# A fused vision tower on one core: whole-tile DMAs for the token tiles, and a reordered tail of gates

## The chip, the cores and the metric

One Trainium2 chip, one of its cores. The time is device microseconds of one execution of the whole kernel; lower is better. Times of several executions are given as a median.

## The reference

The input holds coefficients C of shape (8, 256, 64, 2). Three stages follow one another, all in float32:

```python
h = _L0_tok_ref(x, log_dt, log_w_real, w_imag, 512)          # (8, 256, 512): 2*Re(Cm . exp(K)), a state-space kernel
h = h + _L0_attn_ref(_layernorm(h), w_q, w_k, w_v, w_o)      # 16 query heads, 4 key/value heads of 128, rope, causal
h = h + _L0_ffn_ref(_layernorm(h), select_weight, ...)       # per token one of 8 experts
```

The last stage, for every token and each of 8 experts, divides the squared products with `select_weight` by the squared length of the token minus `select_mean_diff`, passes the score through a sigmoid (the gate), takes the expert with the largest gate, and gives `(1 - gate) * x + gate * (bias + degen @ (upd @ (x - debias)))`.

## The kernel before

There are NB = 8 sequences ("batches") of S = 256 tokens with D = 512 channels. Tokens lie on partitions: a batch has TT = 2 token tiles of 128 tokens x 512 channels, and `x[:, t, b, :]` in on-chip memory is tile t of batch b. **The token order is not the plain one.** Partitions 0 to 63 of tile t hold tokens t*64 to t*64+63, partitions 64 to 127 hold tokens 128 + t*64 and on: `half_rows(hh)` names the partitions of a half and `tokens_of(hh, t)` its tokens. A half is contiguous in `out[b]`; a whole tile is two such runs, 64 tokens apart. In DRAM scratch, `x_dram`, a token's 8 batches stand side by side, so a row of 2 KB (512 float32) is the contiguous piece there.

**Mixing stage (to about 98 us).** Sixteen steps q make the state-space outputs: GpSimd and VectorE build factors, TensorE multiplies, ScalarE evacuates to one of two staging buffers `st[s]` (`evacuate`), and the sync engine writes them to `x_dram` (`store_mixed`, two transfers, line 463). `evacuate` waits until the store of the same buffer two steps earlier has landed (`xd_out[s]`). After the eighth step tile 0 of batch 0 is loaded back (`load_tokens`, line 467), and after each of the next seven steps tile 0 of one more batch; tile 1 of all eight batches follows once the sixteenth store has landed. `load_tokens(t, b, done)` issues two DMAs, one for each half. VectorE waits for `x_early`, `x_first`, `x_second`, `x_third` and `x_rest` before it takes the layer-norm statistics of the tiles they cover; `x_rest` covers batches 3 to 7, both tiles (`dve.wait_ge(x_rest, ...)` ahead of `norm_stats(tokens(3), 3)`, whose instruction is line 1202). Between the tile-1 loads of batches 2 and 3 stand two loads of the output weights (`load_raw(KC)`, `load_raw(KC + 1)`).

**Attention.** For each of 4 groups of heads, 8 batches: projections, rope, scores, softmax, values, output product, each float32 product made of three products of rounded parts (lines 1547 to 1549). Each engine has its own hand-written order of work, with semaphores between them.

**Gates and results.** In the last group's steps the gates of the earlier batches are made two steps behind, and `finish(bb)` (line 1391, VectorE) adds the last term to the two tiles of a result and raises `out_ready`. Results are stored by the sync engine, `store_tile` and `store_half` (line 387), two DMAs of 128 KB a tile, in one fixed order: first all loads of saved values (`load_vs`), then batches 0 to 5, tile by tile, then tiles of batch 7 and of batch 6, of which the sync engine stores the lower halves and ScalarE's queue the upper ones.

**Tail (from about 765 us).** The seventh and eighth batches' (bb = 6, 7) gates are made together in `late_both`, with 4 tiles' worth of columns. VectorE's order was: statistics and normalising of batch 7 tile by tile (`last_stats`, `last_apply`, the latter line 1513), with `finish(4)` for tile 0 between; `gate_choice(5)`; then, once TensorE has the products (`f_ready`), `read_gates` (three instructions, lines 1316 to 1319), `gate_scores` (lines 1339 to 1347), `finish(4)` for tile 1 while ScalarE makes the exponentials (line 931), and `gate_values` and `gate_choice` (lines 1360 to 1377). TensorE then transposes the choices and makes four update products (line 1683), and VectorE ends with two additions for batch 7 (line 1532) and six `finish` instructions. GpSimd makes the reciprocal roots of batch 7's two tiles (lines 739, 741) and then adds batch 5's scaled tiles (`add_scaled`, line 730). At the end the sync engine waits until every store has landed.

Of the kernel before, what the change touches and what calls it, by code (L numbers as in the profile page):

```python
# [25 lines left out]
P = 128  # L26
# [122 lines left out]
def tower(nc, mix_c, mix_s, log_dt, log_wr, w_im, w_qkv, w_o, w_gate, w_gmul, w_upd, centers, slopes, consts, out):  # L149
# [3 lines left out]
    with top:  # L153
# [223 lines left out]
        def half_rows(hh):  # L377

            return slice(hh * NS, (hh + 1) * NS)

        def tokens_of(hh, t):

            first = hh * P + t * NS
            return slice(first, first + NS)

        def store_half(engine, bb, t, hh):
            engine.dma_start(out[bb, tokens_of(hh, t), :], x[half_rows(hh), t, bb, :]).then_inc(stored, 16)

# [36 lines left out]
        def _(sp):  # L425
# [37 lines left out]
                    sp.dma_start(rows[q, hh], st[s][:, hh, :, :]).then_inc(xd_out[s], 16)  # L463

            def load_tokens(t, b, done):
                for hh in range(2):
                    sp.dma_start(x[half_rows(hh), t, b, :], x_dram[tokens_of(hh, t), b, :]).then_inc(done, 16)

            with sp.Fori(0, NQ // 4) as it:
                for s in range(2):  # L470
# [67 lines left out]
            load_vs(3, 1, 3)  # L538
            load_ffn()
            load_vs(3, 3, NB)  # L540
            def store_tile(bb, t, counted, halves=range(2)):
                sp.wait_ge(out_ready, counted)
                for hh in halves:
                    store_half(sp, bb, t, hh)

            with sp.Fori(0, NB - 2) as bb:
                for t in range(TT):
                    store_tile(bb, t, bb * 2 + (t + 1))
            for k, bb in enumerate((NB - 1, NB - 2)):
                for t in range(TT):  # L550
                    store_tile(bb, t, 2 * (NB - 2 + k) + t + 1, (0,))
            sp.wait_ge(stored, 16 * 2 * NB * TT)


        @block.gpsimd
        def _(pool):
# [171 lines left out]
            def add_scaled(bb, t):  # L728
                pool.wait_ge(xn_scaled, bb * 2 + (t + 1))
                nc.gpsimd.tensor_tensor(x[:, t, bb, :], x[:, t, bb, :], norm_set(NB + bb)["xn"][:, t, :],  # L730
                                        ALU.add).then_inc(xn_added, 1)

            normalise_probs(NG * NB - 1)
            norm(2 * NB - 2)
            for t in range(TT):
                mem = norm_set(2 * NB - 1)
                rstd = mem["rstd"][:, t:t + 1]
                pool.wait_ge(tile_var, t + 1)
                nc.gpsimd.tensor_tensor(rstd, mem["mv"][:, t, 1:2], cst[:, C_EPS:C_EPS + 1], ALU.add).then_inc(tile_eps, 1)
                pool.wait_ge(tile_eps, t + 1)  # L740
                nc.gpsimd.tensor_tensor(rstd, rstd, cst[:, C_POW:C_POW + 1], ALU.pow).then_inc(tile_rstd, 1)
            for t in range(TT):
                add_scaled(NB - 3, t)
            pool.wait_ge(x7_added, 2)
            for t in range(TT):
                add_scaled(NB - 2, t)
# [3 lines left out]
        def _(act):  # L750
# [253 lines left out]
            round_probs(last)  # L1004
            round_attn(last, 0)

            def scale_normed(bb):
                mem = norm_set(NB + bb)
                act.wait_ge(gate, bb * GATE + GATE_KEEP)
                for t in range(TT):  # L1010
                    nc.scalar.activation(mem["xn"][:, t, :], mem["xn"][:, t, :], ACT.Copy,
                                         scale=mem["one_minus"][:, t:t + 1]).then_inc(xn_scaled, 1)

            gate_exp(NB - 3)
            xt2(NB - 2)
            scale_normed(NB - 3)
            act.wait_ge(f_ready, NB - 1)
            for t in range(TT):
                act.wait_ge(xt_ready, 2 * (2 * NB - 1) + t + 1)
# [15 lines left out]
        def _(dve):  # L1035
# [226 lines left out]
                return v.tensor_tensor(columns_of_pair(xt_l, q, t), pair_of(bank), columns_of_pair(xt_h, q, t).bitcast(F32),  # L1262
                                       ALU.subtract)

            dve.wait_ge(x_early, 32)
            norm_stat(tokens(0), 0)
            wait_apart(dve, ln_st, 1, 4)
            v.bn_aggr(norm_set(0)["mv"][:, 0, :], stats[:, 0, :]).then_inc(early_var, 1)
# [2 lines left out]
            for q in range(2):  # L1271
                dve.wait_ge(early_hi, q + 1)
                half_rest(q, 0, 5 + q).then_inc(early_lo, 1)
            dve.wait_ge(x_first, 32)
            norm_stat(tokens(0), 1)
            wait_apart(dve, ln_st, 2, 4)
            v.bn_aggr(norm_set(0)["mv"][:, 1, :], stats[:, 1, :]).then_inc(ln_var, 1)
# [2 lines left out]
            for q in range(2):  # L1280
                dve.wait_ge(xt_hi, q + 1)
                half_rest(q, 1, (7, 3)[q]).then_inc(xt_lo, 1)
            dve.wait_ge(x_second, 64)
            norm_stats(tokens(1), 1)
            norm_apply(tokens(1), 1)
            def kq_rest(s, j):
# [2 lines left out]
                v.tensor_tensor(flat(kl), part(kq), flat(kh).bitcast(F32), ALU.subtract).then_inc(kq_lo, 1)  # L1289

            rope(0, 0)
            dve.wait_ge(x_third, 64)
            norm_stats(tokens(2), 2)
            rope(0, 1)
            rope_add(0, 0)
# [26 lines left out]
            def gate_link(bb, n):  # L1322

                def then(ins):
                    n[0] += 1
                    ins.then_inc(gate, 1)
                    dve.wait_ge(gate, bb * GATE + n[0])
                return then

            def bc(t, tiles):  # L1330
                return t.unsqueeze(2).to_broadcast([P, tiles, NE])
# [18 lines left out]
            def gates(bb, mem=None, tiles=TT):  # L1350
                gate_values(bb, mem, tiles)
                gate_choice(bb, mem, tiles)

            def gate_values(bb, mem=None, tiles=TT):

# [10 lines left out]
            def gate_choice(bb, mem=None, tiles=TT):  # L1366

                mem, n = mem or norm_set(NB + bb), [GATE_KEEP]
                then = gate_link(bb, n)
                z, rank, mm, best, first = mem["z"], mem["rank"], mem["mm"], mem["best"], mem["first"]  # L1370
                then(v.tensor_tensor(rank, z, bc(best, tiles), ALU.is_equal))
                then(v.tensor_tensor(rank, rank, cst[:, C_RANK:C_RANK + NE].unsqueeze(1).to_broadcast([P, tiles, NE]),
                                     ALU.mult))
                then(v.tensor_reduce(first, rank, AX.X, ALU.max))
                onehot = mm[:, :, 64:72]
                then(v.tensor_tensor(onehot, rank, bc(first, tiles), ALU.is_equal))
                v.tensor_tensor(mm[:, :, 0:64].rearrange("p t (n h) -> p t n h", n=NE),
                                mem["gm"].rearrange("p t (n h) -> p t n h", n=NE),
                                onehot.unsqueeze(3).to_broadcast([P, tiles, NE, HE]), ALU.mult).then_inc(m_ready, 1)
                assert n[0] == GATE, n  # L1380
# [93 lines left out]
            rope_add(1, 1)  # L1474
            probs_rest(0)
            rope(1, 2)
            dve.wait_ge(x_rest, 16 * 4 * 5)
            norm_stats(tokens(3), 3)
            rope_add(1, 2)
            norm_apply(tokens(3), 3)  # L1480
# [40 lines left out]
            finish(NB - 4, (2, 3), (0,))  # L1521
            last_apply(1)
            gate_choice(NB - 3)
            dve.wait_ge(f_ready, NB)
            read_gates(late_both, quad[:, 0:2, :].rearrange("p b (t c) -> p (b t) c", t=TT), 2 * TT)
            dve.wait_ge(f_read, NB - 1)
            gate_scores(NB - 2, late_both, 2 * TT)
            finish(NB - 4, (2, 3), (1,))
            gates(NB - 2, late_both, 2 * TT)
            mem = norm_set(2 * NB - 1)  # L1530
            for t in range(TT):
                v.scalar_tensor_tensor(x[:, t, NB - 1, :], mem["xn"][:, t, :], mem["one_minus"][:, t:t + 1],
# [412 lines left out]
```

## Time and profile before

| | us |
|---|---|
| median of 3 runs | 802.74 (802.38 to 805.21) |
| profiled execution, its own time | 801.88 |
| its span, first to last instruction | 800.0 |
| TensorE busy | 736.1 (92% of the span) |
| VectorE busy | 575.0 (72%) |
| ScalarE busy | 444.9 (56%) |
| GpSimd busy | 434.4 (54%) |
| mean granted TensorE clock | 0.994 of full speed |

The profiled execution is one run; what lies outside its span is 1.9 us. Times inside it are counted from the span's start. "SPq" and "ACTq" are the queues on which the sync engine and ScalarE issue DMAs; a transfer's issue there is short, and its data lands later. In the views of DMA, q1 is the sync engine's queue and q10 ScalarE's, and the share is that of the time of the core's 16 DMA engines.

### The profile page before, as it was taken

The page shows a single profiled execution, that of the slowest core. Times are in us where ns is not written, and L with a number is a line of the kernel's source. Part 1 is how long each engine was busy: PE and PEld are TensorE (multiplying, and loading weights), DVE is VectorE, ACT ScalarE, POOL GpSimd, SP SyncE. Part 2 cuts the span into 40 slices and gives each one's busy share as a digit, 9 for nine tenths or more (in the row PEclk, how much of TensorE's full clock was granted, in tenths as well). Part 3 has the DMA queues.
Part 4 walks back from the last instruction along what each step waited for, and adds up shares of the span by engine and source line. Part 5 has one row for each costly group of instructions (what it writes and reads, how often), then busy time and mean ns, then how long its engine had stood idle before and what let it go on. Part 6 is the DMA issues. An engine that isn't in the chain of part 4 may idle for free.

```text
span 800.0 us, 19498 instructions
## 1 busy us (share of the span) xinstructions
PE 736.1 (92%) x6902; PEld 671.3 (84%) x6902; DVE 575.0 (72%) x1604; ACT 444.9 (56%) x1236; POOL 434.4 (54%) x649
## 2 busy tenths in 40 slices
PE   0277788999999999999999999999999999999996
PEld 0166768999999999999989999999999998989883
DVE  7999877887765666766674565665666678888886
ACT  6735435665555667555674555555575655465431
POOL 1488866644444747544474564444384745665632
PEclk9999999999999999999999999999999999999999
DMA  9023741100010203000011020000020000000403
GB/s 217 6 56 79 178 138 34 54 8 2 7 47 8 67 8 99 7 7 7 7 29 39 1 93 8 7 7 1 8 68 7 29 8 8 7 7 13 100 1 105
DMA packets 38127, 31.59 MB, mean 39 GB/s; under 512 B 23790, under 2 KB 29294, under 8 KB 38070
## 3 DMA queue, kind: packets, MB, share of 16 engines
q1 hardware_dynamic: 37606, 30.25, 14.3%
q8 instruction: 35, 0.57, 0.3%
q10 hardware_dynamic: 464, 0.59, 0.3%
q14 instruction: 22, 0.18, 0.1%
HBM read 20.34 MB, written 10.49 MB: 39 GB/s over the span
## 4 chain that ended last, share of the span: by engine, by line
PE 81%; DVE 7%; POOL 4%; ACT 3%; issue 2%; DMA 1%; DVEq 0%; SPq 0%; ACTq 0%; POOLq 0%
PE bank_quad L1548 17%; PE bank_quad L1547 16%; PE bank_quad L1549 16%; PE bank_pair L1547 4%; PE bank_pair L1548 4%; PE bank_pair L1549 4%; PE bank_quad L1559 2%; PE bank_pair L1736 2%; PE bank_pair L1746 2%; PE bank_quad L1665 2%; PE bank L1746 2%; PE bank L1750 2%; PE bank L1547 2%; PE bank L1548 2%; PE bank L1549 1%
## 5 line engine op out<-in xcount | busy, mean ns | idle before, releaser
L1547 PE MATMUL bank_quad<-xt_hi,w_hi 128*128 128x256 f32 (+1 forms) x568 | 159.5, 281 | 0.0
L1548 PE MATMUL bank_quad<-xt_hi,w_lo 128*128 128x256 f32 (+1 forms) x568 | 158.9, 280 | 0.0
L1549 PE MATMUL bank_quad<-xt_lo,w_hi 128*128 128x256 f32 (+1 forms) x568 | 158.6, 279 | 0.0
L652 POOL TENSOR_TENSOR swap<-swap,cst 128x512 f32<-128x512 f32 (+1 forms) x96 | 105.5, 1110 | 38.4 <-ACT swap L885 38.3
L942 ACT ACTIVATE sm<-sm,mx 128x128 f32<-128x128 f32 (+1 forms) x256 | 113.6, 445 | 20.1 <-DVE mx L1406 20.1
L1249 DVE TENSOR_TENSOR kq<-kq,swap 128x512 f32<-128x512 f32 (+1 forms) x96 | 89.9, 957 | 25.9 <-POOL swap L652 24.8
L1547 PEld LDWEIGHTS bank_quad<-xt_hi,w_hi 128*128 128x128 f32 x568 | 106.8, 188 | 0.0
L1548 PEld LDWEIGHTS bank_quad<-xt_hi,w_lo 128*128 128x128 f32 x568 | 106.7, 188 | 0.0
L1549 PEld LDWEIGHTS bank_quad<-xt_lo,w_hi 128*128 128x128 f32 x568 | 106.3, 187 | 0.0
L692 POOL TENSOR_SCALAR sm<-sm,rinv 128x128 f32<-128x128 f32 (+1 forms) x256 | 103.9, 418 | 0.1
L954 ACT ACTIVATE ot_hi<-bank_quad 128x512 fp32r<-128x512 f32 x64 | 37.8, 597 | 118.4 <-PE bank_quad L1549 118.4
L419 POOL TENSOR_TENSOR spare<-cst 1x1 f32<-1x1 f32 x70 | 14.2, 203 | 159.2 <-DVE rinv L1418 151.0
L657 POOL TENSOR_TENSOR kq_lo<-kq,kq_hi 128x256 fp32r<-128x256 f32 x93 | 67.4, 751 | 51.4 <-ACT kq_hi L893 51.4
L1243 DVE TENSOR_TENSOR kq<-bank_quad,cst 128x512 f32<-128x512 f32 (+1 forms) x78 | 50.1, 642 | 59.1 <-ACT swap L885 58.7
L884 ACT ACTIVATE swap<-bank_quad 64x512 f32<-64x512 f32 (+1 forms) x78 | 43.4, 556 | 77.9 <-PE bank_quad L1549 77.0
L1397 DVE TENSOR_TENSOR ot_lo<-bank_quad,ot_hi 128x512 fp32r<-128x512 f32 x64 | 43.4, 678 | 23.5 <-ACT ot_hi L954 23.4
L1547 PE MATMUL bank_quad<-wo_hi,ot_hi 128*128 128x512 f32 x132 | 55.0, 416 | 0.4 <-DVE ot_lo L1397 0.4
L1549 PE MATMUL bank_quad<-wo_lo,ot_hi 128*128 128x512 f32 x132 | 51.9, 393 | 0.0
L1548 PE MATMUL bank_quad<-wo_hi,ot_lo 128*128 128x512 f32 x132 | 51.5, 390 | 0.0
L1549 PE MATMUL bank_pair<-wo_lo,ot_hi 128*128 128x512 f32 x124 | 48.2, 389 | 0.0
L1547 PE MATMUL bank_pair<-wo_hi,ot_hi 128*128 128x512 f32 x124 | 48.2, 389 | 0.0
L1548 PE MATMUL bank_pair<-wo_hi,ot_lo 128*128 128x512 f32 x124 | 48.2, 389 | 0.0
(347 smaller groups left out, 2133.9 us busy)
## 6 DMA issues: line engine op xcount, KB each, us to landing
mixed<-st SPq DMA_DIRECT2D x32, 128.0 KB, 2.0
x<-mixed SPq DMA_DIRECT2D x32, 128.0 KB, 3.0
out<-x SPq DMA_DIRECT2D x28, 128.0 KB, 2.3
raw<-in_w_qkv SPq DMA_DIRECT2D x8, 384.0 KB, 3.7
raw<-in_w_o SPq DMA_DIRECT2D x10, 256.0 KB, 2.8
norm_mem<-in_w_qkv SPq DMA_DIRECT2D x6, 384.0 KB, 4.2
later_v<-v_next SPq DMA_DIRECT2D x16, 128.0 KB, 1.7
v_next<-later_v SPq DMA_DIRECT2D x16, 128.0 KB, 2.0
```

What stands on the lines that cost most here:

```text
L652: nc.gpsimd.tensor_tensor(view(sw), view(sw), table(sinT), ALU.mult).then_inc(rot_sin, 1)
L657: nc.gpsimd.tensor_tensor(flat(kl), part(kq), flat(kh).bitcast(F32), ALU.subtract).then_inc(kq_lo, 1)
L692: last = nc.gpsimd.tensor_scalar(sm[:, j, cols], sm[:, j, cols], rinv[:, 2 * j + t:2 * j + t + 1], 1.0, ALU.mult, ALU.mult)
L884: nc.scalar.activation(view(sw)[0:64], src[64:128], ACT.Copy)
L942: last = nc.scalar.activation(sm[:, j, cols], sm[:, j, cols], ACT.Exp, scale=-1.0, bias=mx[:, n:n + 1], accum_out=rsum[:, n:n + 1])
L954: nc.scalar.activation(by_rows(oth, j), natural(banks[first_bank + j]), ACT.Copy).then_inc(ot_hi, 1)
L1243: v.tensor_tensor(view(kq), src, table(cosT), ALU.mult).then_inc(kq_cos, 1)
L1249: v.tensor_tensor(view(kq), view(kq), view(sw), ALU.add).then_inc(kq_rot, 1)
L1397: v.tensor_tensor(by_rows(otl, j), natural(banks[first_bank + j]), by_rows(oth, j).bitcast(F32), ALU.subtract).then_inc(ot_lo, 1)
L1547: mmul(dst, lh, rh, start=start and k == 0, stop=False, skip_group_check=True)
L1548: mmul(dst, ll, rh, start=False, stop=False, skip_group_check=True)
L1549: last = mmul(dst, lh, rl, start=False, stop=stop and k == n - 1, skip_group_check=True)
```

## The change

1. `load_tokens` issues one DMA for a whole tile (256 KB) where it issued two of 128 KB. The DRAM side is now written with three dimensions, 2 halves x 64 tokens x 512 channels; the on-chip side is 128 partitions x 512. All 16 loads change, and the waits' counts are halved.
2. The stores of batches 0 to 5 likewise: one DMA a tile, 12 in place of 24. The stores of batches 6 and 7 stay in halves, on two queues.
3. VectorE's tail: for the last two batches the two instructions on the squared roots (`ssq`) come ahead of the wait for `f_ready`; the third of the three reads (`gm`) comes after the last instruction ahead of the exponentials; `finish(4)` for tile 1 comes after the gates in place of before them.
4. GpSimd's tail: batch 5's first tile is added between the two roots, its second only after `last_apply(1)` is done. ScalarE scales the first of these tiles ahead of `xt2(6)` in place of after it.

```diff
+        def tokens_of_tile(rows, t):
+            return rows.rearrange("(hh t r) d -> t hh r d", hh=2, t=TT)[t]
+
+        def store_tile(engine, bb, t):
+            engine.dma_start(tokens_of_tile(out[bb], t), x[:, t, bb, :]).then_inc(stored, 16)
...
             def load_tokens(t, b, done):
-                for hh in range(2):
-                    sp.dma_start(x[half_rows(hh), t, b, :], x_dram[tokens_of(hh, t), b, :]).then_inc(done, 16)
+                sp.dma_start(x[:, t, b, :], tokens_of_tile(x_dram[:, b, :], t)).then_inc(done, 16)
...
             with sp.Fori(0, NB - 2) as bb:
                 for t in range(TT):
-                    store_tile(bb, t, bb * 2 + (t + 1))
+                    sp.wait_ge(out_ready, bb * 2 + (t + 1))
+                    store_tile(sp, bb, t)
...
-            sp.wait_ge(stored, 16 * 2 * NB * TT)
+            sp.wait_ge(stored, 16 * ((NB - 2) * TT + 2 * 2 * TT))
...
-            for t in range(TT):
-                add_scaled(NB - 3, t)
+            last_norm(0)
+            add_scaled(NB - 3, 0)
+            last_norm(1)
+            pool.wait_ge(tile_xn, 2)
+            add_scaled(NB - 3, 1)
...
             gate_exp(NB - 3)
+            scale_normed(NB - 3, (0,))
             xt2(NB - 2)
-            scale_normed(NB - 3)
+            scale_normed(NB - 3, (1,))
...
+            def last_squares(bb, mem):
+                then = gate_link(bb, [0])
+                then(v.tensor_tensor(mem["ssq"], mem["rstd"], mem["rstd"], ALU.mult))
+                then(v.scalar_tensor_tensor(mem["ssq"], mem["mv"][:, :, 1], float(D), mem["ssq"], ALU.mult, ALU.mult))
+
+            def last_scores(bb, mem, f, tiles):
+                n = [2]
+                then = gate_link(bb, n)
+                score, z, gu = mem["score"], mem["z"], mem["gu"]
+                v.tensor_tensor(gu, f[:, :, 0:64], cw[:, 0:64].unsqueeze(1).to_broadcast([P, tiles, 64]), ALU.subtract)
+                v.scalar_tensor_tensor(score, f[:, :, 64:72], -2.0,
+                                       cw[:, 64:72].unsqueeze(1).to_broadcast([P, tiles, NE]), ALU.mult,
+                                       ALU.add).then_inc(f_read, 1)
+                dve.wait_ge(f_read, bb + 1)
+                v.tensor_tensor(gu, gu, gu, ALU.mult)
+                then(v.tensor_tensor(score, score, bc(mem["ssq"], tiles), ALU.add))
+                v.tensor_reduce(z, gu.rearrange("p t (n s) -> p t n s", n=NE), AX.X, ALU.add)
+                then(v.reciprocal(score, score))
+                then(v.tensor_tensor(z, z, score, ALU.mult))
...
+                v.tensor_tensor(mem["gm"], f[:, :, 72:FC], cw[:, 72:FC].unsqueeze(1).to_broadcast([P, tiles, 64]),
+                                ALU.subtract)
...
             gate_choice(NB - 3)
+            dve.wait_ge(gate, (NB - 2) * GATE)
+            last_squares(NB - 2, late_both)
             dve.wait_ge(f_ready, NB)
-            read_gates(late_both, quad[:, 0:2, :].rearrange("p b (t c) -> p (b t) c", t=TT), 2 * TT)
-            dve.wait_ge(f_read, NB - 1)
-            gate_scores(NB - 2, late_both, 2 * TT)
+            last_scores(NB - 2, late_both, quad[:, 0:2, :].rearrange("p b (t c) -> p (b t) c", t=TT), 2 * TT)
+            gates(NB - 2, late_both, 2 * TT)
             finish(NB - 4, (2, 3), (1,))
-            gates(NB - 2, late_both, 2 * TT)
```

For comparison, the one other load whose DRAM side is written with an outermost dimension of 2 onto 128 partitions is that of `log_dt` at the start (line 426); `log_wr` beside it, of the same 64 KB, is plain (line 758, ScalarE's queue):

```python
sp.dma_start(lg[:, 0, :], log_dt.rearrange("(hh h) -> hh h", hh=2).unsqueeze(1).to_broadcast([2, NS, P])).then_inc(par_in, 16)
nc.scalar.dma_start(lg[:, 1, :], log_wr).then_inc(par_in, 16)
```

## Rows read from the trace of the kernel before

**Rows 1.** The page: the chain that ended last, shares of the span.

```profile
PE 81%; DVE 7%; POOL 4%; ACT 3%; issue 2%; DMA 1%; DVEq 0%; SPq 0%; ACTq 0%; POOLq 0%
```

**Rows 2.** Timeline of the sync engine's queue: start, length (us), transfers.

```profile
76.12 1.21 SPq L467 DMA_DIRECT2D x<-mixed  x2
...
101.09 3.98 SPq L467 DMA_DIRECT2D x<-mixed  x6
```

**Rows 3.** Chain of waits around the first tiles' loads: start, length.

```profile
98.79 2.23 DMA mixed<-st
...
104.65 0.70 DVE stats L1202
```

**Rows 4.** Timeline of VectorE where the last loads are used.

```profile
137.09 1.28 DVE L1202 BATCH_NORM_STATS2 stats<-x 128x6 f32<-128x512 f32 x2
```

**Rows 5.** Timeline of the sync queue (SPq): the stores of the results.

```profile
738.01 7.89 SPq L387 DMA_DIRECT2D out<-x  x9
...
778.80 18.66 SPq L387 DMA_DIRECT2D out<-x  x12
...
796.85 0.61 SPq L387 DMA_DIRECT2D out<-x  x1
```

**Rows 6.** Chain of waits and two groups in the tail's gate part.

```profile
L1513 DVE TENSOR_SCALAR late_xn<-x,late_both x2: 546/1013/1480, 775.8 to 778.9; 128x512 f32<-128x512 f32 x2
...
778.82 2.68 POOL L730 TENSOR_TENSOR x<-x,late_xn 128x512 f32<-128x512 f32 x2
...
779.80 0.60 ACT L1020 ACTIVATE norm_mem<-bank_quad 128x512 f32<-128x512 f32 x1 [1.29 <-PE bank_quad L1665]
...
780.43 0.66 PE bank_pair L1872 x4
...
783.00 0.42 DVE late_both L1316
...
783.53 0.34 DVE late_both L1319
...
784.91 0.08 DVE late_both L1342
...
785.24 0.36 DVE late_both L1344
...
786.31 0.75 DVE x L1391
...
788.90 0.44 DVE late_both L1377
...
794.07 0.75 DVE x L1391
```

**Rows 7.** Transfers by name; DMA at 2.1 to 2.5 us, log_dt under way.

```profile
x<-mixed SPq DMA_DIRECT2D x32, 128.0 KB, 3.0
...
GB/s 0 256 51 205 205 205 256 154 256 103 154 308 154 205 51 154 52 102 102 52 102 0 0 102 0 102 0 102 0 0 102 0 102 0 102 0 0 102 0 102
...
q10 hardware_dynamic: 60, 0.03, 22.4%
q1 hardware_dynamic: 27, 0.01, 11.3%
...
0.73 0.71 SPq L426 DMA_DIRECT2D lg<-in_log_dt  x1
```

**Rows 8.** DMA in 125.8 to 126.3 us: 2 KB packets, MB, share of 16 engines.

```profile
q1 hardware_dynamic: 68, 0.14, 71.3%
```

**Rows 9.** The same in 99.7 to 100.3 us: 256-byte packets of the mixed stores.

```profile
q1 hardware_dynamic: 533, 0.13, 105.9%
```

**Rows 10.** DMA, 77.3 to 77.9 us in 40 slices: the first load begins.

```profile
DMA  0000000000009940300309497090303800390300
```

**Rows 11.** The same in 779.9 to 780.5 us: 2 KB packets of half stores.

```profile
q1 hardware_dynamic: 60, 0.12, 89.2%
```

**Rows 12.** DMA in 0 to 6 us in 40 slices: the highest rate.

```profile
GB/s 0 0 0 0 0 0 0 0 0 0 0 3 89 174 171 58 58 147 195 96 158 133 158 38 122 108 35 63 296 371 368 368 283 453 424 301 387 428 384 356
```

More of the change, by code:

```diff
@@ L540, in _ @@
             load_vs(3, 3, NB)
[L541 to L544, printed above, removed]
             with sp.Fori(0, NB - 2) as bb:
                 for t in range(TT):
-                    store_tile(bb, t, bb * 2 + (t + 1))
+                    sp.wait_ge(out_ready, bb * 2 + (t + 1))
+                    store_tile(sp, bb, t)
             for k, bb in enumerate((NB - 1, NB - 2)):
                 for t in range(TT):
-                    store_tile(bb, t, 2 * (NB - 2 + k) + t + 1, (0,))
-            sp.wait_ge(stored, 16 * 2 * NB * TT)
+                    sp.wait_ge(out_ready, 2 * (NB - 2 + k) + t + 1)
+                    store_half(sp, bb, t, 0)
+            sp.wait_ge(stored, 16 * ((NB - 2) * TT + 2 * 2 * TT))
         @block.gpsimd
@@ L734, in _, with last_norm @@
             norm(2 * NB - 2)
-            for t in range(TT):
+            def last_norm(t):
                 mem = norm_set(2 * NB - 1)
@@ L741, in _ @@
                 nc.gpsimd.tensor_tensor(rstd, rstd, cst[:, C_POW:C_POW + 1], ALU.pow).then_inc(tile_rstd, 1)
-            for t in range(TT):
-                add_scaled(NB - 3, t)
+            last_norm(0)
[3 more added lines that the diff above has]
+            add_scaled(NB - 3, 1)
             pool.wait_ge(x7_added, 2)
@@ L1005, in _, with scale_normed @@
             round_attn(last, 0)
-            def scale_normed(bb):
+            def scale_normed(bb, tiles=range(TT)):
                 mem = norm_set(NB + bb)
                 act.wait_ge(gate, bb * GATE + GATE_KEEP)
-                for t in range(TT):
+                for t in tiles:
                     nc.scalar.activation(mem["xn"][:, t, :], mem["xn"][:, t, :], ACT.Copy,
@@ L1263, in half_rest @@
                                        ALU.subtract)
-            dve.wait_ge(x_early, 32)
+            dve.wait_ge(x_early, 16)
             norm_stat(tokens(0), 0)
@@ L1273, in _ @@
                 half_rest(q, 0, 5 + q).then_inc(early_lo, 1)
-            dve.wait_ge(x_first, 32)
+            dve.wait_ge(x_first, 16)
             norm_stat(tokens(0), 1)
@@ L1282, in _ @@
                 half_rest(q, 1, (7, 3)[q]).then_inc(xt_lo, 1)
-            dve.wait_ge(x_second, 64)
+            dve.wait_ge(x_second, 32)
             norm_stats(tokens(1), 1)
@@ L1291, in _ @@
             rope(0, 0)
-            dve.wait_ge(x_third, 64)
+            dve.wait_ge(x_third, 32)
             norm_stats(tokens(2), 2)
@@ L1352, in gates @@
                 gate_choice(bb, mem, tiles)
+            def last_squares(bb, mem):
[16 more added lines that the diff above has]
+                then(v.tensor_tensor(z, z, score, ALU.mult))
+                then(v.tensor_tensor(z, z, ctr[:].unsqueeze(1).to_broadcast([P, tiles, NE]), ALU.subtract))
+                then(v.tensor_tensor(z, z, slp[:].unsqueeze(1).to_broadcast([P, tiles, NE]), ALU.mult))
+                assert n[0] == GATE_Z
+                v.tensor_tensor(mem["gm"], f[:, :, 72:FC], cw[:, 72:FC].unsqueeze(1).to_broadcast([P, tiles, 64]),
+                                ALU.subtract)
             def gate_values(bb, mem=None, tiles=TT):
@@ L1476, in _ @@
             rope(1, 2)
-            dve.wait_ge(x_rest, 16 * 4 * 5)
+            dve.wait_ge(x_rest, 16 * 2 * 5)
             norm_stats(tokens(3), 3)
```

## The prediction

> **What bounds the kernel now.** I read the chain that ended last first: TensorE holds 81% of it and DMA 1% [rows 1]. So a change to transfers can give little, and can only cost much if it makes a transfer late. The next view is the sync engine's queue, to see where a transfer is waited for. Tile 0 of batch 0 is asked for at 76.12, the tile-1 loads from 101.09 on, 0.66 us an issue [rows 2]. The chain runs through that place: the last mixed store takes 2.23 us from 98.79, the first tile-1 load follows, and VectorE begins on it at 104.65 [rows 3]. The last load wait (`x_rest`, ten transfers after the change) is passed in time: VectorE's statistics start at 137.09 and nothing there waits for data [rows 4]. At the end the stores decide. A backlog of batches 0 to 3 goes out from 738.01, batch 4 begins at 778.80, and the sync engine's last store is issued at 796.85, 3.15 us before the span ends at 800.0, while VectorE's last instruction starts at 794.07 [rows 5, 6]: the queue is some 2 us behind VectorE.
>
> **The compute part of the tail.** Three steps, all in VectorE's chain [rows 6].
> - `last_apply(1)`, line 1513, took 1480 ns where its twin took 546: GpSimd's additions, from 778.82 on, ran beside it. After the change they are kept away from it, so it ends 0.93 us earlier. TensorE began its transposes on it at 780.43. Then ScalarE's evacuation is last, which frees the first tile's columns from 779.80 to 780.40 once the product before is done; the new products can start at 780.45, where before they stood behind the transposes at 780.43 + 0.66 = 781.09. That is 0.63 us. GpSimd's second addition now falls on `gate_choice(5)`, which it also did before; that is ready well ahead of `f_ready`. The first addition runs beside an instruction that reads PSUM, and I cost it at nothing.
> - Of the gate chain, the `gm` read (0.34) and the stretch from 784.91 to 785.24 (0.33, second square and score sum) leave the path. The squares are two short instructions in the wait that ends at 783.00, and I cost them at nothing; if `f_ready` came as they start they would cost about what they save.
> - In the exponentials' wait stood a `finish` of 0.75; now stands `gm`, 0.42: 0.33 less. Sum 1.00, with the 0.63 1.63 us. The `finish` itself comes back after the choice, so VectorE's last six instructions move up by some 0.9 only. And its store, which could be issued at 786.31 + 0.75 = 787.06, now comes after the choice: 788.90 + 0.44 = 789.34, less 1.63 plus 0.75 is 788.45. TensorE's filler products and the four updates then limit the end, at about 1.05 earlier.
>
> **The transfers.** Two issues become one. If nothing else changed, the front would win 0.4 us (one issue of 0.66 less, a little more data), and the end 2.9: four half stores of batch 5 become two, the queue has caught up, and the last issue stands at about 794.0. But I expect something else. The new DRAM side has an outermost dimension of 2. One transfer of the trace has the same form onto 128 partitions, that of `log_dt`, issued at 0.73. In the stretch where it is the only one of the sync queue, q1 has 27 packets of 512 bytes in 11.3% of the time of 16 engines, 1.8 engines' worth, while the plain `log_wr` has 60 packets in 22.4% [rows 7]. In the second half of that window the rate comes in single slices of 102 GB/s, 9 of them in 20 slices of 10 ns, with zeros between. A slice of 102 GB/s is 1 KB, two packets at once, each 22 ns: two engines in step and fourteen idle. The issue took 0.71 us.
>
> Taken over: a merged tile is 128 packets of 2 KB, 64 on each of two engines, where the half transfer has 4 on each of 16.
>
> The Trainium skill ("DMA: Bandwidth & Descriptors", section on why a DMA increments its semaphore by 16) states this as a rule: the engines used are the largest number up to 16 that divides the outermost size of both sides, and on the sync queue always the lowest-numbered ones; for 2 and 128 that is 2. The trace agrees for `log_dt`, and no row shows the rule for a store. By the opposite, 16 engines, the sum is that of the first rival.
>
> **Prices.** A 2 KB packet: 0.713 x 16 x 500 ns / 68 = 83.9 ns [rows 8]. A merged transfer then takes L = 64 x 83.9 = 5.37 us of the two engines. Bounds: the highest rate, 453 GB/s over 16 engines [rows 12], gives 72 ns and L = 4.6; four times the 26.8 ns of `log_dt`'s packets (0.113 x 16 x 400 / 27) gives 107 ns and L = 6.9. I take rows 8, same packet size and no crowding. A pair of mixed stores puts 64 packets of 256 bytes on every engine: 1.059 x 16 x 600 / 533 = 19.1 ns, S = 1.22 us [rows 9]. From issue to first data 1.4 us: 76.12 to the thirteenth slice, 77.48 [rows 10]. From last data to landing: 2.23 less 1.4 less 0.6 is about 0.3 [rows 3]; for a store to the result, 3.15 less 1.4 less 0.34 is 1.4.
>
> **The front.** I take it that all merged transfers use the same two engines, and that these serve the queue in order. Then they carry 8 loads and 8 pairs of stores (steps 9 to 16) without a pause from 77.5: 8 x 5.37 + 8 x 1.22 = 52.7, to 130.2, landed 130.5, where before it was 101.0. ScalarE's evacuations wait for these stores, so the mixing stage stretches with them; its own period of (98.79 - 76.12) / 7 = 3.2 us is below the 6.6 of the engines. The tile-1 loads start moving at 131.9. The first lands at 137.6, 33 us later than before. All eight, with two weight loads between (16 packets an engine, 1.3 us), end at 131.9 + 43.0 + 1.3 = 176.2, landed 176.5. VectorE passed this wait at 137.09, so **everything behind is 39.4 us late**; the lateness of the earlier loads lies inside that. If the engines shared their time between transfers instead of taking them in order, the stores would land earlier and the sum of bytes up to `x_rest` would be the same, so only 2 to 3 us of this hang on the order. Nothing wins it back, as TensorE is the bound from there on.
>
> **The end**, in times of before. The backlog of batches 0 to 3 is 8 merged stores from 739.4: to 782.4. Batch 4's first tile to 787.7. Its second is issued at 788.45, moves at 789.85, ends 795.2; batch 5's tiles end at 800.6 and 806.0. Behind them on the same two engines stand four half stores, 4 packets each: 807.3, landed 808.7. That is **8.7 us later** than 800.0, and the 1.05 us that VectorE wins lie hidden under it. No row shows a store of this form; the bound from rows 11, 0.892 x 16 x 600 / 60 = 143 ns a packet with all engines at work, is the third rival.
>
> Sum against the profiled execution: 801.88 + 39.4 + 8.7 = **850.0 us**. The median of the runs is 802.74, 0.9 above that execution; I leave it at 850. Differences below 0.5% (4 us) can't be told from none here. With L = 4.6 the front gives 27.1 and the end 6.4, 835; with L = 6.9 the front gives 64 and the end, where the backlog then reaches on, 25: 891.
> TensorE stands idle for long stretches in the front, and its clock may be at the lower level when it resumes. The granted mean was 0.994, 4.8 us lost in all; as much again is the most that I add above.
>
> **Rivals.**
> - *All 16 engines.* The change does what it looks like. 801.9 - 0.4 - 2.9 = 798.6, within 0.5% or just beyond. For it: on-chip side and bytes are plain, and a compiler could reorder the dimensions. Against it: `log_dt` was not spread. It holds if in the new profile the merged loads land in about 3 us. Chance 0.07.
> - *Two engines, but another pair each time.* Then a load is slow and no queue forms: 5 us for the first load, some 3 for stores behind a load on its pair, 5 at the end, about 815. The rows can't exclude it. Chance 0.05.
> - *Stores crowd as half stores do*, 143 ns, 9.1 us each: 739.4 + 12 x 9.1 = 849, plus 2.7, so the end costs 52 and the total is 893. For it: 89% of all engines' time went into 60 packets [rows 11]. Against it: that is with 16 engines at once, and here two. Chance 0.04.
> - *Loads on two engines, stores on all.* For it: only a load shows the form. 801.9 + 39.4 - 2.9 = 838. Chance 0.06.
>
> **How the numbers follow.** The forecast's own case has 0.78, with a range of its own from 835 to 875. The range 834 to 880 takes in the fourth rival and leaves out the first three (0.16) and a little above 880. Slower by over 0.5%: 0.78 + 0.06 + 0.04 + 0.05 = 0.93; the first rival's 0.07 I split into 0.04 for the same and 0.03 for faster.
>
> **What would show it.** Right: the merged loads' median landing far above 3.0 us, up to tens where they queue; the tile-1 loads issued near 130; the chain's DMA share 5% or more; DMA share near 2/16 around 140 to 175; stores still moving some 10 us after VectorE's last instruction; line 1513 at 0.55 us both times. Wrong: a landing of about 3 us at a high rate, with the last load wait passed near 137.

## The result and the profile after

The changed kernel takes 850.87 us (median of 5 runs, 849.01 to 851.73), the kernel before 803.54 in the same session: 1.058 times as long [1.057 to 1.060]. The prediction was 850.0, with a range of 834 to 880. Between the medians the difference is 47.3 us, between the spans of the two profiled executions 48.7. The profiled execution took 850.87, with a span of 848.7, and the mean granted clock of TensorE was 0.962 of full speed (before: 0.994).

The page of the kernel after: busy times, the granted clock and the DMA share in 40 slices, the chain that ended last by engine, and the issues (for the merged transfers the page has no landing time).

```profile
PE 746.5 (88%) x6902; PEld 680.8 (80%) x6902; DVE 573.2 (68%) x1604; ACT 444.9 (52%) x1236; POOL 434.8 (51%) x649
...
PEclk9999676989999999999999999999999999999996
DMA  8032321210000010200001020000010000000113
...
PE 72%; SPq 8%; DVE 6%; DMA 4%; POOL 4%; ACT 2%; issue 2%; DVEq 0%; POOLq 0%; ACTq 0%
...
x<-mixed SPq DMA_DIRECT2D x16, 256.0 KB
...
out<-x SPq DMA_DIRECT2D x12, 256.0 KB
```

In [rows 1] the sync queue had 0% of the chain and DMA 1%. Now they hold 12%, some 100 us, and TensorE's part is 611 us (72% of 848.7) where it was 648 (81% of 800.0): the chain goes through issues and transfers from the first load on. VectorE and ScalarE do the same work as before, and less densely.

The timeline of the sync engine's queue in the front (start, length, transfers), which answers to [rows 2]:

```profile
76.33 0.64 SPq L473 DMA_DIRECT2D x<-mixed  x1
...
80.22 4.56 SPq L470 DMA_DIRECT2D mixed<-st  x2
84.82 2.34 SPq L473 DMA_DIRECT2D x<-mixed  x1
87.21 3.57 SPq L470 DMA_DIRECT2D mixed<-st  x2
...
117.49 3.50 SPq L470 DMA_DIRECT2D mixed<-st  x2
127.53 4.06 SPq L473 DMA_DIRECT2D x<-mixed  x3
...
137.88 21.07 SPq L473 DMA_DIRECT2D x<-mixed  x5
158.99 5.01 SPq L500 DMA_DIRECT2D later_v<-v_next  x1
164.44 1.41 SPq L451 DMA_DIRECT2D raw<-in_w_o  x2
```

A step of the mixing stage now takes (117.49 - 87.21) / 5 = 6.06 us, where it took 3.2, and the tile-1 loads are asked for at 127.53 instead of 101.09. The issue of a transfer itself becomes long: from the third step on the sync engine stands in its own issues. In the chain of waits, each of the last loads' issues takes as long as one transfer:

```profile
120.48 6.98 DMA mixed<-st
...
143.75 5.04 SPq L473
...
153.91 19.24 DMA x<-mixed
```

The DMA view of 142 to 162 us (packets, MB, share of 16 engines), where the sync queue moves nothing but tile loads:

```profile
q1 hardware_dynamic: 506, 1.02, 13.1%
```

13.1% of 16 is 2.1 engines, and 506 packets in 20 us are 2 x 20000 / 506 = 79 ns a packet and engine. 64 of them make 5.06 us, which is the 5.04 of the issues. By the share itself a packet would cost 0.131 x 16 x 20000 / 506 = 83 ns; but two engines are 12.5% of sixteen, so the share counts some 5% too much here.

VectorE's timeline at `x_first`, `x_second` and `x_rest`, which answers to [rows 3] (104.65) and [rows 4] (137.09); in brackets the idle time ahead and what ended it:

```profile
135.13 0.69 DVE L1210 BATCH_NORM_STATS2 stats<-x 128x6 f32<-128x512 f32 x1 [13.43 <-DMA x<-mixed]
...
140.64 1.29 DVE L1210 BATCH_NORM_STATS2 stats<-x 128x6 f32<-128x512 f32 x2 [0.96 <-DMA x<-mixed]
...
173.17 1.28 DVE L1210 BATCH_NORM_STATS2 stats<-x 128x6 f32<-128x512 f32 x2 [3.76 <-DMA x<-mixed]
```

The first wait is passed 30.5 us late, `x_rest` 36.1 us late. Later on the lateness is 38.5: GpSimd starts the same three weight roundings at 413.05 before and at 451.56 after, and the fourth group's last products (line 1700) start at 765.53 and 804.05. The 2.4 us between 36.1 and 38.5 lie where TensorE takes up its work. Busy times of PE, PEld, DVE, ACT and POOL by stretch, then the granted clock, DMA share and GB/s, and below them TensorE's timeline:

```profile
175.00:180.00 5.00, 3.05 (x14) 3.06 (x15) 4.12 (x16) 4.11 (x12) 3.89 (x5) 0.61 0.08 28
180.00:185.00 5.00, 5.00 (x33) 5.00 (x33) 3.66 (x20) 3.32 (x14) 2.16 (x6) 0.70 0.52 161
185.00:190.00 5.00, 5.00 (x45) 5.00 (x44) 3.42 (x5) 3.20 (x6) 4.65 (x10) 1.00 0.00 0
```

```profile
176.95 0.79 PE L1771 MATMUL bank_pair<-kq 128*128 128x128 f32 x2 [3.94 <-POOL kq_lo L660]
```

After 3.94 us without work TensorE resumes at 0.5 of full speed (1.2 GHz). A clock of 0.61 and 0.70 over two stretches of 5 us is 2 x (0.39 + 0.30) x 5 = 6.9 us at half speed; half of that, 3.5 us, is the most that it can have cost. The matmul counts show it too: 33 between 180 and 185, 45 in the next stretch.

The end: the sync queue (to be read beside [rows 5]), and the DMA share in 40 slices of 0.47 us from 830 us to the end:

```profile
776.51 54.12 SPq L391 DMA_DIRECT2D out<-x  x12
830.84 10.18 SPq L394 DMA_DIRECT2D out<-x  x4
```

```profile
DMA  1012599999411111111126897997211111111100
```

VectorE's last `finish` ends at 832.46; data moves until 847.9, for most of it at a share of a tenth, two engines out of sixteen. The chain of waits and VectorE's timeline in the gate part, which answer to [rows 6], with the group of `last_apply`:

```profile
818.98 2.13 PE bank_quad L1700 x16
821.21 0.42 DVE late_both L1373
```

```profile
823.72 0.42 DVE L1386 TENSOR_TENSOR late_both<-bank_quad,cw 128x256 f32<-128x256 f32 x1
...
826.32 0.74 DVE L1426 SCALAR_TENSOR_TENSOR x<-bank_quad,norm,x 128x512 f32<-128x512 f32 x1
...
830.94 1.52 DVE L1426 SCALAR_TENSOR_TENSOR x<-bank_quad,late_both,x 128x512 f32<-128x512 f32 x2
```

```profile
L1548 DVE TENSOR_SCALAR late_xn<-x,late_both x2: 546/546/546, 814.3 to 817.4; 128x512 f32<-128x512 f32 x2
```

### The profile page after: what moved, and what is told of

The parts are those of the page before. It is cut to its first block, busy times and chain, and to the rows that moved or that the text cites. A ratio compares the mean times of both kernels' runs of the same rounds, so it can differ in the third digit from the quotient of the medians.

```text
span 848.7 us, 19447 instructions
## 1 busy us (share of the span) xinstructions
PE 746.5 (88%) x6902; PEld 680.8 (80%) x6902; DVE 573.2 (68%) x1604; ACT 444.9 (52%) x1236; POOL 434.8 (51%) x649
## 4 chain that ended last, share of the span: by engine, by line
PE 72%; SPq 8%; DVE 6%; DMA 4%; POOL 4%; ACT 2%; issue 2%; DVEq 0%; POOLq 0%; ACTq 0%
PE bank_quad L1583 15%; PE bank_quad L1582 15%; PE bank_quad L1584 15%; SPq L473 4%; PE bank_pair L1582 4%; PE bank_pair L1584 4%; PE bank_pair L1583 4%; SPq L470 3%; DMA x<-mixed 2%; PE bank_quad L1700 2%; PE bank_pair L1771 2%; PE bank L1781 1%; PE bank L1785 1%; PE bank_pair L1781 1%; PE bank L1582 1%
## 5 line engine op out<-in xcount | busy, mean ns | idle before, releaser
L1257 DVE TENSOR_TENSOR kq<-kq,swap 128x512 f32<-128x512 f32 (+1 forms) x96 | 87.9, 936 | 24.7 <-POOL swap L655 23.6
L1608 PE MATMUL bank_quad<-cst 128*128 128x512 f32 x26 | 17.7, 828 | 41.7 <-DVE vtab L1125 34.8
```

Of the source, the lines that this page charges most:

```text
L1257: v.tensor_tensor(view(kq), view(kq), view(sw), ALU.add).then_inc(kq_rot, 1)
```

## The experiments

The theory: a DRAM side whose outermost dimension is 2 puts a transfer on two of the sixteen engines, for loads (front, some 38.5 us) and for stores (end, some 10). Against it stood a plain cost of size or of three dimensions, and one of a load or a store alone. The diffs are against the changed kernel, "-" being its lines; where the number of transfers changes, the counts that the waits compare with change too, and those lines are left out.

### Loads back to halves

```diff
-                sp.dma_start(x[:, t, b, :], tokens_of_tile(x_dram[:, b, :], t)).then_inc(done, 16)
+                for hh in range(2):
+                    sp.dma_start(x[half_rows(hh), t, b, :], x_dram[tokens_of(hh, t), b, :]).then_inc(done, 16)
```

> The changed kernel with its loads as two half transfers again, each with an outermost dimension of 64; the stores of batches 0 to 5 stay one transfer a tile. Theory (a whole tile's DRAM side has an outermost dimension of 2 and runs on 2 of 16 engines, loads and stores alike, and the two costs add up): VectorE's statistics on the third batch's tiles start at about 137 as before, the two-engine stores end about 10 us late, in all 812 us, ratio 1.013. Rival A (only the loads run on two engines, the stores are spread; the late end in the changed kernel is a result of the late front): about 800, ratio 0.997. Rival B (the front's loss is another's, and the loads are innocent): 850, ratio 1.058.

Measured: 814.55 us against 803.14, ratio 1.0146 [1.0129 to 1.0163], span 812.4. This execution was already 1.9 us late at `x_rest` (138.97 against 137.09), 1.7 of it before a tile was loaded (its first load is issued at 77.78, before at 76.12), and stayed so in the middle, and the end adds 812.4 - 800.0 - 1.9 = 10.5. Its sync queue at the end:

```profile
739.88 54.14 SPq L391 DMA_DIRECT2D out<-x  x12
794.24 10.00 SPq L394 DMA_DIRECT2D out<-x  x4
```

The front is as before but for those 1.9 us, and the end as in the changed kernel. So the loads carry the front's loss, the stores the end's, and the form costs a store too.

### Stores back to halves

```diff
-                    store_tile(sp, bb, t)
+                    for hh in range(2):
+                        store_half(sp, bb, t, hh)
```

> The changed kernel with its stores as two half transfers again; the loads stay one transfer a tile. Theory: the front keeps its 36 us and the 2.4 us behind it, the end is not late any more and wins the tail's 1 us: 802 + 38.5 - 1 = 839, ratio 1.047. With the first experiment's loss the two add up to the whole (10 + 38.5 = 48.5). Rival A (the stores cost nothing by themselves): 850, ratio 1.058. Rival C (the loads only cost where the stores are merged too): 801, ratio 0.999.

Measured: 838.92 us, ratio 1.0445 [1.0427 to 1.0462], span 838.2, thus 38.2 over the span before (35.8 between the medians; the profiled execution is the longest of the four). `x_rest` is passed 36.8 us late:

```profile
173.85 1.28 DVE L1211 BATCH_NORM_STATS2 stats<-x 128x6 f32<-128x512 f32 x2 [3.70 <-DMA x<-mixed]
```

With the experiment before, the two losses add up: 0.0146 + 0.0445 = 0.0591, against 0.0584 for both.

### The reordered tail alone

Loads and stores both back to halves, as in the two diffs above.

> The changed kernel with loads and stores both as two half transfers again, so only the reordered tail of VectorE, GpSimd and ScalarE stays. Theory (the order of work wins 0.9 us at VectorE's last instruction, and the sync queue's eight half stores from batch 5 on still set the end, starting about 1 us earlier): 1.0 us less than before, ratio 0.9988. Rival E (the queue's backlog hides the win wholly): 0, ratio 1.000. Rival F (the end follows the gate chain's 1.6 us in full): ratio 0.998.

Measured: 802.69 us against 803.51, ratio 0.9991 [0.9981 to 1.0000]. This is at the edge of no difference; the trace says more. The run's first result store is 1.19 us later than in [rows 5], and VectorE's last pair, which was at 793.21 for 1.61 us:

```profile
793.66 1.52 DVE L1428 SCALAR_TENSOR_TENSOR x<-bank_quad,late_both,x 128x512 f32<-128x512 f32 x2
```

795.18 - 794.82 - 1.19 = -0.83 us. So the reordering gains 0.8 us, and in the changed kernel it is hidden under the stores.

### Merged loads that keep sixteen engines

The scratch is laid out in the order of the tiles, so that a tile is one run of 128 rows; the stores of results stay in halves.

```diff
-            rows = x_dram.rearrange("(hh q m t) c (a j) -> q hh (t c a) m j", hh=2, q=NQ, t=2, j=64)
+            rows = x_dram.rearrange("(u hh q m t) c (a j) -> u hh q (t c a) m j", u=2, hh=2, q=NQ // 2, t=2, j=64)
...
-                sp.dma_start(x[:, t, b, :], tokens_of_tile(x_dram[:, b, :], t)).then_inc(done, 16)
+                sp.dma_start(x[:, t, b, :], x_dram[t * P:(t + 1) * P, b, :]).then_inc(done, 16)
```

> The loads stay one transfer of 256 KB a tile, 16 in place of 32, but the DRAM scratch keeps its rows in the tiles' order, so that a tile is 128 rows in a row and the DRAM side is 128 x 512, outermost dimension 128. Stores as two halves. Theory (the outermost dimension of 2 is the cause, not the size or the number of transfers): the loads land in some 3 us, the last wait is passed near 137, the first tile-1 tile comes 0.4 us earlier than before: with the tail's 1 us about 1.4 less than before, ratio 0.998. Rival G (a transfer of 256 KB from strided rows is slow by its size, or one semaphore step a tile is): the front stays tens of us late, about 839, ratio 1.047.

Measured: 801.28 us, ratio 0.9974 [0.9964 to 0.9984], span 798.9: the fastest kernel of the case that still writes the reference's result. Its load group on the page, and the queue and VectorE at the tile-1 loads:

```profile
x<-mixed SPq DMA_DIRECT2D x16, 256.0 KB, 3.3
```

```profile
103.73 2.92 SPq L473 DMA_DIRECT2D x<-mixed  x5
```

```profile
104.20 0.69 DVE L1211 BATCH_NORM_STATS2 stats<-x 128x6 f32<-128x512 f32 x1
```

The same 256 KB in one transfer lands in 3.3 us, an issue takes 0.5 us, and from the last mixed store's issue to the first statistics pass 104.20 - 98.79 = 5.41 us, where it was 104.65 - 98.35 = 6.30. Size and the count of transfers are thus not the cause. What differs from the changed kernel's load is how the DRAM side is written: 128 x 512 in place of 2 x 64 x 512, so an outermost dimension of 128 for 2, and two dimensions for three. The next run takes up the three dimensions, for a store. At `x_rest` (136.83) 0.3 us of the gain is left, which is within the spread of this wait: the next two runs have the same loads and pass it at 137.22 and 136.59.

### Merged stores with three dimensions and sixteen engines

As the last, and batches 0 to 5 in one transfer a half, both tiles in it (64 x 2 x 512):

```diff
-                for t in range(TT):
-                    sp.wait_ge(out_ready, bb * 2 + (t + 1))
-                    store_tile(sp, bb, t)
+                sp.wait_ge(out_ready, bb * 2 + 2)
+                for hh in range(2):
+                    sp.dma_start(out[bb, hh * P:(hh + 1) * P, :].rearrange("(t r) d -> r t d", t=TT),
+                                 x[half_rows(hh), :, bb, :]).then_inc(stored, 16)
```

> As the one before, and the stores of batches 0 to 5 are one transfer of 256 KB for each half of the partitions, both tiles in it: DRAM side 64 x 2 x 512, on-chip side 64 x 2 x 512, outermost dimension 64. Same size, same number (12) and as many dimensions as the changed kernel's stores. Theory: they are spread over 16 engines, batch 5 needs two issues in place of four, the queue has caught up at the end, and the last half store is issued some 3 us earlier than before: with the front's 0.4 about 3.5 us less than before, ratio 0.9957. Rival H (three dimensions, not the outermost one, make a store slow): the end is late by several us, ratio 1.01. Rival I (batch 5's stores wait for its second tile and the end gains nothing): ratio 0.998.

Measured: 801.85 us, ratio 0.9980 [0.9971 to 0.9989]. The stores of 256 KB land in 3.1 us, so three dimensions don't make a store slow either. With the run before, that leaves the outermost dimension (no run has a load of three dimensions with another outermost one). But the 12 issues that were saved gain nothing. The DMA views of 739.6 to 741.6 us (backlog) and of 793 to 798 us (end):

```profile
q1 hardware_dynamic: 257, 0.49, 96.8%
```

```profile
q1 hardware_dynamic: 465, 0.82, 62.8%
q10 hardware_dynamic: 306, 0.51, 35.5%
```

From 793 to 798 us the engines are taken to 98%, which speaks for them as the limit of the end. It doesn't exclude Rival I, whose 0.998 is what came out: a store now waits for both tiles of its batch, and the sync engine's last issue ends at 797.11, where it was 796.31 in the run before. A packet of these stores from 64 partitions costs 0.968 x 16 x 2000 / 257 = 120 ns.

### Whole-tile stores into plain rows

As the merged loads above, and a tile of batches 0 to 5 goes to 128 rows side by side. The result's rows of these batches stand in another order; bytes and packets are the same.

```diff
-            engine.dma_start(tokens_of_tile(out[bb], t), x[:, t, bb, :]).then_inc(stored, 16)
+            engine.dma_start(out[bb, t * P:(t + 1) * P, :], x[:, t, bb, :]).then_inc(stored, 16)
```

> As the kernel with spread loads (DRAM scratch in the tiles' order), but the stores of batches 0 to 5 are one transfer of a whole tile, written to 128 rows in a row of the result: DRAM side 128 x 512, outermost dimension 128. This puts the rows of these batches into another order, so the result is not the reference's; the transfers are those that the changed kernel's stores would be if they were spread. Theory (the end is bound by the 16 engines' work, as they are 98% busy from 793 to 798 us and a half store's packet takes 143 ns there, because it comes from 64 partitions): packets of whole tiles take about 84 ns, the first 4 of 12 half tiles' worth become cheaper by 60 ns x 16 packets = 0.9 us, and the span is about 1 us less than the spread loads alone, ratio 0.996. Rival J (issues are what holds the end): two issues of 0.75 less, 1.5 to 3 us, ratio 0.9945. Rival K (packets are as slow from 128 partitions): as with spread loads, ratio 0.9974.

Measured: 800.35 us against 803.44, ratio 0.9958 [0.9944 to 0.9971], span 798.3. The stores land in 2.1 us, and in the view of 739.6 to 741.6 us their packets cost less:

```profile
q1 hardware_dynamic: 391, 0.72, 96.6%
```

0.966 x 16 x 2000 / 391 = 79 ns a packet, from 128 partitions, against 120 from 64. From VectorE's last instruction to the span's end it is now 3.87 us, where it was 5.18 before, 5.21 with the merged loads alone and 5.47 in the last run; so these stores gain some 1.3 us at the end. They save issues and engine time together, and Rival J's 0.9945 lies within the interval as well as the theory's 0.996: which of the two it was stays open. This run also prices the first rival, all sixteen engines for loads and stores: 3.1 us less than before in the medians.

### TensorE kept at work through the late load

A filler of ten calls, which the trace counts as 20 products, in TensorE's order ahead of its first steps:

```diff
+            keep_warm(10, 3)
```

> The changed kernel with ten filler products of 512 columns on TensorE (some 8.6 us at full clock) behind the first batch's values, where it otherwise waits for the last loads. It tells what the 2.4 us are by which TensorE falls behind between 173 us and the middle of the kernel. Theory (the granted clock is 0.5 for 6.8 us behind the wait, because the engine stood idle before): the clock stays at 1.0 there, and 2 us come back: 849, ratio 1.056, and the granted clock of 175 to 183 us is 1.0. Rival D (the 2.4 us are lost to transfers or to other engines): 851 or a little more, ratio 1.058 or above, whatever the clock.

Measured: 853.94 us, ratio 1.0644 [1.0621 to 1.0667]: not what was expected. The filler outlasts the wait:

```profile
171.59 8.75 PE L1608 MATMUL bank_quad<-cst 128*128 128x512 f32 x20
```

It ends at 180.34 where work is there at 176.95. The clock does stay at 1.00 from 175 on, but 3.4 us are lost to the filler. So the filler was too long to answer the question; the next run has six calls, 12 products.

```diff
+            keep_warm(6, 3)
```

> The filler experiment again with six products in place of ten, since ten ran until 180.2 us and TensorE's work was ready at 177. Six take 5.2 us and end near 176.8. Theory (clock): the granted clock of 175 to 185 us is 1.0, the kernel's later parts move up by some 1.6 to 2 us against the changed kernel, 849, ratio 1.056. Rival D: the clock stays up and nothing moves, ratio 1.0584.

Measured: 849.61 us, ratio 1.0580 [1.0560 to 1.0599], span 847.1. The windows that answer to those of the result, and GpSimd's landmark of the middle, which is at 451.56 in the changed kernel:

```profile
175.00:180.00 5.00, 5.00 (x33) 3.98 (x32) 4.12 (x16) 4.11 (x12) 3.89 (x5) 1.00 0.08 28
180.00:185.00 5.00, 5.00 (x45) 5.00 (x44) 3.89 (x21) 4.76 (x17) 2.18 (x6) 1.00 0.52 161
```

```profile
449.76 5.05 POOL L568 TENSOR_TENSOR w_lo<-raw,w_hi 128x896 fp32r<-128x896 f32 x2
```

`x_rest` is passed at the same moment (173.16), the clock is 1.00, and the middle comes 1.8 us earlier. How firm that is, other runs tell: from `x_rest` to this landmark it is 275.96 to 276.04 us in the four executions in which no load is late and the clock in between is 1.00 (the kernel before, loads back to halves, merged loads that keep sixteen engines, merged stores with three dimensions), 276.9 in the two in which the clock fell to 0.97 and 0.99 there without a late load, 278.39 in the changed kernel, 278.36 with its stores in halves, and 276.60 here. So of the 2.4 us at least 1.8 were the clock's. Against the changed kernel the total can't be told apart by the ratios, whose intervals overlap.

## Why the prediction was right

**What bounds it.** That a transfer only matters where it becomes late was right: the chain's DMA share is 4% (5% or more was expected), but with 8% of issues beside it, which I had not foreseen as a form in which the delay would show.

**The number of engines.** This step decided everything and held: `log_dt`'s 27 packets [rows 7] showed two engines, and the tile loads do the same (13.1% of 16 engines). The Trainium skill ("DMA: Bandwidth & Descriptors", section on why a DMA increments its semaphore by 16) gives it as a rule, and the runs agree on both sides of it: 2 as outermost dimension, 1.02 MB in 20 us; 64 or 128, landings of 2.1 to 3.3 us for the same bytes. That loads and stores use the same two engines is borne out by the step of 6.06 us, close to 5.05 + 1.22, though it is even a little less. That it is the same pair each time shows in the rate, which stays at two engines' worth while five loads are queued.

**The price L.** 5.37 us was forecast, 5.05 measured (79 ns a packet for 83.9). Most of that lies in how rows 8 were read: by the share, which counted 5% too much where it could be compared with two full engines, and 83.9 less 5% is 80. The mixing stage's half of it shows: its last store lands at 127.46, forecast 130.5. From the first tile-1 data to `x_rest` the same should have shrunk by 2.5 us, and shrank by 0.3. Of the 2.2 between, 0.8 lie in the first load, which starts slowly, by the DMA view of 128.8 to 130.4 us:

```profile
q1 hardware_dynamic: 24, 0.05, 12.6%
```

24 packets in 1.6 us, where 79 ns a packet and engine make 40; so 0.6 us. Of the rest, 0.45 lie in the second load (135.13 to 140.64, 5.51) and 0.8 in the last five with their weight loads (145.80 to 173.17, 27.4, for 5 x 5.06 + 1.3 = 26.6). Their cause stays open; no run took them apart. So the front is 36.1 late, 3.3 less than forecast.

**The clock.** It was allowed for ("as much again") and not in the sum: 2.4 us. With it the lateness is 38.5 where 39.4 was forecast; two errors of opposite sign make the agreement look better than the steps are.

**The end.** 8.7 us was forecast, 10.2 measured (848.7 - 800.0 - 38.5). The order of events is as predicted: the backlog runs out (at 825), batch 4's second tile is issued at 827.25, in times of before 788.75 for 788.45, and three merged stores and the halves follow on the two engines. Two terms were missing. Four of the half stores are ScalarE's, and they too have 4 packets on each of the two engines, 1.3 us. And the first of the three starts slowly again. The DMA views of 828 to 831 us, where its data begins at 828.4, and of 844 to 847:

```profile
q1 hardware_dynamic: 36, 0.07, 11.1%
```

```profile
q1 hardware_dynamic: 78, 0.15, 13.2%
```

In 2.6 us 36 packets for 65 at the steady rate, 1.2 us lost. The sum made again: 828.4 + 3 x 5.06 + 32 x 0.079 + 1.2 = 847.3, and the last data moves at 847.9. The third rival's price, 143 ns a packet, appears nowhere on the two engines: 12 us from 800 on carry 304 packets, 79 ns each.

**The total.** 39.4 + 8.7 = 48.1 us was forecast, and 48.7 lie between the two spans: 3.3 too much in the front, 2.4 for the clock and 1.5 at the end too little. So it is partly luck that the total came out this close; that two engines carry the merged transfers, and where they are waited for, came out as reasoned.

**The compute part of the tail.** `last_apply` takes 546 ns both times, as forecast. The new products start at 818.98, in times of before 780.48 (forecast 780.45), yet `f_ready` comes only 0.3 us earlier and not 0.63. The forecast took their old start as 781.09, where the chain of waits has the transposes end; TensorE's timeline shows that they had begun at 780.92, before and after:

```profile
780.92 2.04 PE L1665 MATMUL bank_quad<-raw,norm_mem 128*128 128x136 f32 x16
818.98 2.12 PE L1700 MATMUL bank_quad<-raw,norm_mem 128*128 128x136 f32 x16 [0.25 <-ACT norm_mem L1028]
```

So the start gains 0.44; 0.08 go to a longer run and 0.07 to VectorE's answer (0.11 us for 0.04). The gate chain and the exponentials' wait gave 1.14 where 1.00 was forecast (6.32 us from `f_ready` to the end of the choice, now 5.18): the choice ends at 826.39, 1.43 us earlier than 789.32 + 38.5 (forecast 1.63). VectorE's end is 0.86 us earlier there and 0.83 with the tail alone, for 0.9.

**The rivals.** None came. The first, had it been so, would have been 3.1 to 3.3 us faster as priced, but its reason, that the end's 2.9 us come from fewer issues, is not borne out: with issues saved and stores from 64 partitions nothing came (ratio 0.9980 against 0.9974 without), and of the 1.3 us that came with stores from 128 partitions the runs don't tell the issues' part from the packets'. The fourth rival's 838 lies beside the 838.92 of the run in which only the loads were merged by chance, since it counts on merged stores that gain 2.9, and there they were in halves.

## What to carry to other kernels

Before two transfers are joined into one, look at the outermost dimension of both sides: a tile read as 2 x 64 x 512 kept two engines busy for 5.05 us, while read as 128 x 512 it went over all sixteen and landed in 3.3; in the trace a DMA share near 2/16 with full-size packets is the sign of it. If the layout of a scratch is one's own, lay it out so that the piece to be read is one run; that brought a front 38.5 us late back to the old one, with half the loads issued. And where transfers set the end, price them by the packet, and count what every queue still has to send.

## What was unexpected

- An issue on the sync queue is not always short: while the two engines were full, loads took up to 5.14 us to issue, a result store 6.68 and one of the four half stores 8.23 (0.5 to 0.6 us otherwise), and everything behind them on that engine waited.
- A transfer that uses all engines waits for the slowest two as well. The value store (`later_v`) and two weight loads issued at 158.99 and 164.44 had most engines free, yet needed 14.5 and 9.8 us to land, where the page of the profile gives 1.7 and 3.1 for their kind. From 166 us on the trace shows bursts of up to 437 GB/s until 168.3, and then only 41 to 55, two engines' worth, until 172: what they had on the other engines had gone through. The DMA view of 162 to 166 us:

```profile
raw<-in_w_o SPq DMA_DIRECT2D x2, 256.0 KB, 9.8
later_v<-v_next SPq DMA_DIRECT2D x1, 128.0 KB, 14.5
```

- After a pause the two engines started slowly (24 packets for 40 in the first 1.6 us, 36 for 65 in 2.6 us), while the sync engine was still issuing what came behind. What held them is not shown.
- A 2 KB packet cost 79 ns on two engines, 79 ns on sixteen when the stores came from 128 partitions, and 120 ns when they came from 64. The Trainium skill ("SBUF — State Buffer", section "Door 1: The DMA port swizzle") has it that 64 neighbouring partitions reach only half of the 16 ports through which DMAs reach the on-chip memory, and gives some 218 GB/s for them where 128 partitions have 436. In the two views above the runs agree in direction, with 246 GB/s against 358, and not in size, perhaps because halves on both sides were under way at once; no run here had stores of one half alone. It isn't the whole cause: in the last stretch of the run with whole-tile stores (793 to 798 us), where half stores from both queues make up most of the 734 packets, a packet costs 0.734 x 16 x 5000 / 734 = 80 ns.
- GpSimd's second addition, moved away from `last_apply`, runs beside `gate_choice(5)`, and a small instruction of it takes 1.26 us where its neighbours take 0.2, beginning 0.04 us after the addition and ending with it. It was so before too (line 1371, 1.24 us at 780.29), and costs nothing either time, since `f_ready` comes later. VectorE's timeline:

```profile
818.07 1.26 DVE L1407 TENSOR_TENSOR late_fifth<-late_fifth,cst 128x16 f32<-128x16 f32 x1
```

and GpSimd's:

```profile
818.03 1.27 POOL L733 TENSOR_TENSOR x<-x,late_xn 128x512 f32<-128x512 f32 x1 [0.66 <-DVE late_xn L1548]
```
